# TensorE reads the expert weights at addresses held in registers, from a table of expert numbers

## The reference

```
x = x + attention(ctx, layernorm(x), Wq)      # q, k = both times Wq; v = k; causal softmax
y = layernorm(x)
gates = softmax(y @ gate_W); the two largest of 8, normalized, are cw
out = y;  for e in 0..7: out += cw[:, e] * (relu(y @ W1[e] + b1[e]) @ W2[e] + b2[e])
x = x + out
```

## Time and profile before

| | us |
|---|---|
| median of 2 runs | 143.59 (143.34 and 143.83) |
| span of the profiled execution | 142.0 |
| PE busy | 128.8 |
| PEld busy | 95.9 |
| DVE busy | 107.1 |
| ACT busy | 98.0 |
| POOL busy | 56.3 |

### The profile page before, as it was taken

How to read it: one execution, slowest core, us unless ns; L and a number is a source line. 1 busy time by engine, 2 the same in 40 slices (tenths; PEclk the granted TensorE clock), 3 DMA queues, 4 the chain that set the end, 5 groups by cost and what they waited for, 6 DMA issues and landing times. The chain is left out here.

```text
span 142.0 us, 3307 instructions
## 1 busy us (share of the span) xinstructions
PE 128.8 (91%) x1181; PEld 95.9 (67%) x1181; DVE 107.1 (75%) x422; ACT 98.0 (69%) x205; POOL 56.3 (40%) x66
## 2 busy tenths in 40 slices
PE   6789739989999989999999899999998999699992
PEld 2369528567887656867886568787975667567781
DVE  0748989997749799498568897677497994978573
ACT  3136636788894966778949686789867848689940
POOL 6591953033038943303097730330327603333500
PEclk9999985699999999999999999999999999999999
DMA  3998020000002000200020000200000002000002
GB/s 109 314 283 269 10 76 5 0 0 2 0 7 71 0 2 5 74 0 5 0 74 0 7 0 2 78 0 0 2 5 0 0 5 74 0 2 5 0 0 74
DMA packets 9904, 5.54 MB, mean 39 GB/s; under 512 B 504, under 2 KB 9888, under 8 KB 9888
## 3 DMA queue, kind: packets, MB, share of 16 engines
q1 hardware_dynamic: 9744, 5.27, 13.0%
q10 hardware_dynamic: 144, 0.07, 0.2%
HBM read 4.28 MB, written 1.05 MB: 38 GB/s over the span
## 5 line engine op out<-in xcount | busy, mean ns | idle before, releaser
L653 POOL TENSOR_TENSOR h_lo<-h,h_hi 128x512 f16<-128x512 f32 x24 | 27.8, 1159 | 67.1 <-ACT h L536 67.1
L536 ACT ACTIVATE h<-psH,b1T 128x512 f32<-128x512 f32 x64 | 43.4, 686 | 2.7 <-PE psH L368 1.8
L535 ACT ACTIVATE h_hi<-psH,b1T 128x512 f16<-128x512 f32 x48 | 33.0, 687 | 10.3 <-PE psH L368 10.2
L821 DVE SCALAR_TENSOR_TENSOR acc<-psY,weight_y,acc 128x128 f32<-128x128 f32 x125 | 35.1, 342 | 4.2 <-PE psY L389 3.3
L805 DVE TENSOR_TENSOR h_lo<-h,h_hi 128x512 f16<-128x512 f32 x24 | 17.3, 721 | 15.2 <-ACT h L536 15.2
L364 PE MATMUL psH<-x_hi,w_hi 128*128 128x512 f16 x62 | 24.0, 387 | 0.2 <-ACT h L536 0.2
L368 PE MATMUL psH<-x_lo,w_hi 128*128 128x512 f16 x62 | 23.8, 384 | 0.4
L365 PE MATMUL psH<-x_hi,w_lo 128*128 128x512 f16 x62 | 23.8, 385 | 0.0
L389 PE MATMUL psY<-w_hi,h_hi 128*128 128x128 f16 x192 | 22.7, 219 | 0.0
L389 PE MATMUL psY<-w_lo,h_hi 128*128 128x128 f16 x192 | 22.7, 219 | 0.0
L389 PEld LDWEIGHTS psY<-w_hi,h_hi 128*128 128x128 f16 x192 | 15.4, 98 | 3.3
(11 more groups left out here) (211 smaller groups left out, 209.6 us busy)
## 6 DMA issues: line engine op xcount, KB each, us to landing
w_sb<-in_L_ffn_W_dram SPq DMA_DIRECT2D x8, 256.0 KB, 4.5
ctx_sb<-in_ctx_dram SPq DMA_DIRECT2D x4, 256.0 KB, 2.7
x_sb<-in_x_dram SPq DMA_DIRECT2D x1, 768.0 KB, 6.5
out_dram<-acc SPq DMA_DIRECT2D x3, 256.0 KB, 2.2
x_sb<-in_x_dram SPq DMA_DIRECT2D x1, 256.0 KB, 3.5
out_dram<-acc SPq DMA_DIRECT2D x2, 128.0 KB, 1.8
wq_sb<-in_L_xattn_Wq_dram ACTq DMA_DIRECT2D x1, 64.0 KB, 2.7
b_rows<-in_L_ffn_b_dram SPq DMA_DIRECT2D x3, 4.0 KB
```

Of the source, the lines that this page charges most:

```text
L535: nc.scalar.activation(h_hi[:, C * (e % 2) + c, :], psH[c][:, :], ACT.Relu, bias=bias, scale=scale)
L536: nc.scalar.activation(h[:, C * (e % 2) + c, :], psH[c][:, :], ACT.Relu, bias=bias, scale=scale).then_inc(h_ready, 1)
L653: nc.gpsimd.tensor_tensor(h_lo[:, i, :], h[:, i, :], h_hi[:, i, :], ALU.subtract).then_inc(hlo0_ready, 1)
L821: last = nc.vector.scalar_tensor_tensor(out=o, in0=y, scalar=weight_y[:, t, e:e + 1], in1=o, op0=ALU.mult, op1=ALU.add)
```

## The change

A table `order` in SBUF holds the numbers 0 to 7 in every partition; GpSimd writes it once by an iota, after its other constants. For each expert of groups 1, 2 and 3 the hidden product on PE first waits for the table (order_ready), loads entry e of it from SBUF into a register (`value_load`, with bounds 0 to 7), and keeps the value in `experts[e]`. The stationary operands of the six hidden matmuls are then slices of w1_hi and w1_lo, seen flat, that start at the value times 256 plus 0 or 128. The moving operands of the output product are slices of w2_hi, w2_lo or w2_sb, seen flat, at the same value times 256 (C * D) plus 0 or 128. Group 0 keeps its fixed addresses. Since the table is in order, the same weights are read as before, in the same order. The slice for the output product is built by `chosen_weights` at each matmul.

```diff
--- before.py
+++ after.py
@@ -104,6 +104,7 @@
         ident = sb("ident", [P, P])
         ident16 = sb("ident16", [P, P], fp16)
         mask = sb("mask", [P, P])
+        order = sb("order", [P, E], i32)
         restart = sb("restart", [P, TG, E])
         half = sb("half", [P, TILES])
         warm = sb("warm", [P, 4 * P], fp16)
@@ -201,6 +202,7 @@
         uT_ps, uT_ready, attn_ps = sem("uT_ps"), sem("uT_ready"), sem("attn_ps")
         x1_ready, var2_ready, rstd2_ready = sem("x1_ready"), sem("var2_ready"), sem("rstd2_ready")
         xf_ready, xfT_ps, xhi_ready, xlo_ready = sem("xf_ready"), sem("xfT_ps"), sem("xhi_ready"), sem("xlo_ready")
+        order_ready = sem("order_ready")
         base_ready = sem("base_ready")
 
         logits_ps, below_ready, gate_exp_ready = sem("logits_ps"), sem("below_ready"), sem("gate_exp_ready")
@@ -352,20 +354,31 @@
                                             start=True, stop=True)
                 last.then_inc(b2_ps, 1)
 
+            experts = {}
+
             def hidden_product(g, e):
 
                 u = (g * E + e) * C
                 if e == 0:
                     pe.wait_ge(xhi_ready, (g + 1) * TG)
                 pe.wait_ge(w1lo_ready, e // 2 + 1)
+                first = 0
+                if g > 0:
+                    pe.wait_ge(order_ready, 1)
+                    experts[e] = pe.value_load(order[0:1, e:e + 1], min_val=0, max_val=E - 1)
+                    first = experts[e] * HID
+                    hi_flat, lo_flat = (v[:, :, :].rearrange("p e h -> p (e h)") for v in (w1_hi, w1_lo))
                 for c in range(C):
                     pe.wait_ge(h_ready, u + c - 1)
                     w = slice(c * P, (c + 1) * P)
-                    nc.tensor.matmul(psH[c][:, :], w1_hi[:, e, w], x_hi[:, g, :], start=True, stop=False)
-                    nc.tensor.matmul(psH[c][:, :], w1_lo[:, e, w], x_hi[:, g, :], start=False, stop=False)
+                    hi, lo = w1_hi[:, e, w], w1_lo[:, e, w]
+                    if g > 0:
+                        hi, lo = (v[:, bass.ds(first + c * P, P)] for v in (hi_flat, lo_flat))
+                    nc.tensor.matmul(psH[c][:, :], hi, x_hi[:, g, :], start=True, stop=False)
+                    nc.tensor.matmul(psH[c][:, :], lo, x_hi[:, g, :], start=False, stop=False)
                     if e == 0 and c == 0:
                         pe.wait_ge(xlo_ready, (g + 1) * TG)
-                    nc.tensor.matmul(psH[c][:, :], w1_hi[:, e, w], x_lo[:, g, :], start=False,
+                    nc.tensor.matmul(psH[c][:, :], hi, x_lo[:, g, :], start=False,
                                      stop=True).then_inc(z_ps, 1)
 
             def output_product(g, e):
@@ -381,12 +394,18 @@
                 pe.wait_ge(y_used, n + 1)
                 last_expert = n_is_last(g, e)
 
+                def chosen_weights(weights, c):
+                    if g == 0:
+                        return weights[:, e, c, :]
+                    flat = weights[:, :, :, :].rearrange("p e c n -> p (e c n)")
+                    return flat[:, bass.ds(experts[e] * (C * D) + c * D, D)]
+
                 def add_product(t, hidden, weights, start, stop):
 
 
                     o = LAST_BANKS[t][:, 0:D] if last_expert else tiles(psY[i])[:, t, :]
                     for c in range(C):
-                        last = nc.tensor.matmul(o, hidden[:, C * i + c, t * P:(t + 1) * P], weights[:, e, c, :],
+                        last = nc.tensor.matmul(o, hidden[:, C * i + c, t * P:(t + 1) * P], chosen_weights(weights, c),
                                                 start=start and c == 0, stop=stop and c == C - 1)
                     if stop and (last_expert or t == TG - 1):
                         last.then_inc(y_ps, 1)
@@ -621,6 +640,8 @@
             nc.gpsimd.memset(b2_cat[:, :], 0.0).then_inc(const_ready, 1)
             pool.wait_ge(const_ready, 4)
 
+            nc.gpsimd.iota(order[:, :], [[1, E]], base=0, channel_multiplier=0).then_inc(order_ready, 1)
+
             def attention_rstd(a, ts):
                 v = slice(ts[0], ts[-1] + 1)
                 pool.wait_ge(var2_ready, a * TG + ts[-1] + 1)
```

## The result

| | before | after |
|---|---|---|
| median of 2 runs, us | 143.59 | 145.83 (145.67 and 146.0) |
| ratio, 95% interval | | 1.0158 (1.0109 to 1.0208) |
| span of the profiled execution, us | 142.0 | 143.9 |

The changed kernel is 2.2 us slower. The forecast was 153.5 us, 9.9 over before, in a range of 143.5 to 185. The direction holds, the size is over four times too large, and of the rivals "hidden" (144.4) lies nearest.

The account below looks back on a forecast made before the run. TensorE's array time was taken as the bound (busy 128.8 of 142.0 us). Sequencer work of 3.46 us against 2.63 per split expert gave 5.0 us in group 3 and 4.8 in groups 1 and 2: 153.5 us, range 143.5 to 185.

Parts of the forecast that it names:

- hidden: Rival, chance 0.26: sequencer work fits under the array if a register-addressed matmul costs at most 0.04 us; 144.4 us.
- A matmul with a register address: 0.08 us: PE's sequencer, 30 instructions per split expert: 0.08 us each, 0.092 for the pair with its fixed partner.
- The 146.5 us worked out with it: Side estimate outside the sum: at the firmware's price, 0.29 us excess per split expert, about 146.5 us.
- Load 0.4 us: PE's sequencer, once per expert of groups 1 to 3: loading one number from SBUF to a register takes 0.4 us.
- 10 register instructions of 0.03 us, 0.3 in all: PE's sequencer, per expert: wait, load, multiply and 8 operand addresses, counted as 10 instructions, 0.3 us.
- The queue can't bank much.: Between experts: little lead carries over, since chunk 1 of the last group's hidden product already starts 0.04 us late.
- output matmuls 0.09 us apart: Sign of being right, groups 1 to 3: output matmuls start some 0.09 us apart instead of 0.0555.
- PE is idle with no engine named before a hidden product for some tenths: Sign of being right: before each hidden product PE idles some tenths of a us, no engine named (issue).
- expert 5 has the xf transposes with 0.64 us of idle: covered: Groups 1 and 2: 0.64 us of idle before expert 5's xf transposes hides its sequencer excess, so no loss.
- Iota at nothing, the wait for the table at nothing: GpSimd's iota hides in a 1.81 us wait for VectorE; PE's table wait is met some 50 us early; no cost.
- Anew, 179 us: Rival, chance 0.26 (with much dearer): each of 30 matmuls computes its own address, two register instructions each; 179 us.
- Clock: Rival, chance 0.04: PE fed with gaps loses its upper clock level; over group 3 alone 20 us, 164 us.

Follow-up runs that it names:

- the kernel with the table alone: Against the changed kernel: iota and PE's wait for the table stay, no number is loaded, every address is fixed; 143.84 us, ratio 0.9985 to the kernel before.
- the doubled load: Against the changed kernel: a second load and bounds check directly behind the first, its value used for the output product; 157.79 us, ratio 1.095 to the kernel before.
- addresses worked out anew: Against the changed kernel: each output matmul works out its own address by a register instruction, hidden ones not; 179.16 us, ratio 1.2459 to the kernel before.

## Why the prediction was wrong in size

- **A matmul with a register address: 0.08 us. The step that failed.** It was the largest term: 30 times 0.092 = 2.76 of the 3.46 us per split expert. The output matmuls still start 0.0555 apart, taking their register addresses away gains nothing (146.13 us), and a run of 8 such pairs goes out in next to no time. With it gone, the sequencer's work per split expert is about 1.9 us (load, check and 8 addresses, with the pauses, and its waits), under the 2.63 of the array. The bound from below, 0.012 us, holds; I had taken a value from a row of another engine. Of the Trainium skill's page "TensorE: Matmul & The Clock Gate" (section "Step-by-step: what each phase is for") I had weighed the firmware's 62 ns per MATMUL: register addresses do not fall back on that here. The 146.5 us worked out with it is nearer to the result than any rival, by luck: it puts 0.29 us on every ordinary split expert, where none is lost.
- **Load 0.4 us**: 0.30, and 0.36 from start to start. Right, but for the first one (0.49).
- **10 register instructions of 0.03 us, 0.3 in all**: an address is 0.1 us with its pause, and the bounds check of 0.29 us wasn't counted at all. About 1.05 us for check and 8 addresses, over three times my 0.3. The errors partly cancelled.
- **"The queue can't bank much."** Wrong: 0.93 us of matmuls lie handed out when the wait for the table is passed, in an ordinary expert. That covers the chain of 0.85 us. The lead looks like a count and not a time: 17 MATMULs and 16 LDWEIGHTS are still to start then, at 129.88 in front of fp16 matmuls (0.93 us) and at 118.25 in front of an fp32 product (2.2 us) alike. Where it comes from wasn't tested.
- **Where the cost stands.** The sign "output matmuls 0.09 us apart" failed, and so did "the last group grows most, per expert": 0.60 us once. "PE is idle with no engine named before a hidden product for some tenths" came true, but behind transposes that wait for VectorE (two of attention, one of the gate). These I had entered as cover ("expert 5 has the xf transposes with 0.64 us of idle: covered"). That is the reverse of what they are: the unmet wait held the sequencer as well as the array (transposes at 124.50, the next register instruction at 124.507), so what is behind it starts with no lead.
- **Iota at nothing, the wait for the table at nothing**: right for the iota, and for the wait where no load follows, shown by the kernel with the table alone. In front of a load the wait is 0.11 of the chain's 0.85 us.
- **Hidden, 144.4 us**: the nearest of the cases, with the right condition on the matmul's price; its remainder of small losses before hidden products was too small, as it had two register instructions there and not the whole chain of 0.85 us.
- **Anew, 179 us**: 179.16 when built, by other terms. **Clock**: stayed up here, fell with the doubled load and with addresses worked out anew.

## What to carry to other kernels

To use an address from a register cost TensorE's matmuls nothing here; what costs is the chain from the load to the first address, 0.85 us with 0.29 of it a bounds check, and each further address, 0.1 us, and they cost only where the sequencer has no lead. The places without lead were, but for the first load, those behind PE's own unmet waits: find them in PE's waits, and put loads ahead of them, behind a long run of matmuls. In this kernel PE's idle time for data was no cover for its own sequencer.

## What the runs showed of the hardware that wasn't expected

- PE's sequencer was ahead of the array by 17 MATMULs and 16 LDWEIGHTS (0.93 us of 128-column fp16 matmuls), and regained that lead fast: 8 pairs in under 0.02 us.
- From the end of one register instruction of PE to the start of the next it is about 0.06 us (0.08 where a matmul's instructions stand between), longer than the 32 ns that an address takes; a load from SBUF is 0.30 us (the first 0.49), the bounds check 0.15 and 0.02.
- Waits that are already met cost 51 ns and the pause when they stand alone before a register instruction, as the wait for the table does at 129.88.
- With two loads per expert, PE was busy 1.65 us between 131 and 135, and from 135 to 138 the granted clock was at the 1.2 GHz level, with PE then fully busy.
